# Handing out the sort's pieces beside the mean layer by their duration instead of by their number

## What is computed

```python
def _L0_gnn_ref(feature, src, dst, W):
    msgs = feature[src]
    summed = jax.ops.segment_sum(msgs, dst, num_segments=N_NODES)
    deg = jax.ops.segment_sum(jnp.ones_like(dst, dtype=feature.dtype), dst, num_segments=N_NODES)
    agg = summed / jnp.maximum(deg, 1.0)[:, None]
    return jax.nn.relu(agg @ W.T) + feature
...
def _L1_gnn_ref(x, edge_index, ...):
    nodes = jnp.concatenate([src, dst]); nbr = jnp.concatenate([dst, src])
    order = jnp.lexsort((nbr, nodes))
    nbrs = nbr[order].reshape(N, deg)
    h = _layer(h, nbrs, ...)          # uses w = _evolution_row(deg, tr, ti)
```

## Time and profile before

| | |
|---|---|
| median of 3 runs | 10004.24 us (9991.14 to 10006.8) |
| profiled execution, first to last instruction (its span) | 9988.2 us |
| profiled execution's own time | not listed apart from the span; the span lies 16.0 us under the median and within the spread of the runs but for 2.9 us |
| busy share of the span | PE 78%, DVE 80%, ACT 60%, POOL 70% |
| first gather of the mean issued | 366.7 us |
| last gather of the mean issued | 2516.4 us |

### The profile page before, as it was taken

The page is one execution under the profiler, slowest core; times in us unless marked ns, Lnnn a source line. Parts: engine busy times, 40 slices in busy tenths (PEclk is TensorE's granted clock), DMA queues, the critical chain, the costliest instruction groups (busy, mean ns, idle before and its releaser), DMA issues.

```text
span 9988.2 us, 178573 instructions
## 1 busy us (share of the span) xinstructions
PE 7824.2 (78%) x39865; PEld 6121.3 (61%) x39865; DVE 7971.0 (80%) x24833; ACT 5963.0 (60%) x18344; POOL 6961.9 (70%) x7476
## 2 busy tenths in 40 slices
PE   4444555555799999898889989888888888848887
PEld 4333444444477777777677777666666666636665
DVE  7787556555878887999967768788888888899999
ACT  6777777777877774111100006688888888846665
POOL 0466777777078887777678877566666666649995
PEclk6555555555899999999999999855565565557876
DMA  2222222222588888887766662322222222210000
GB/s 52 54 48 48 53 53 53 53 53 53 189 253 239 243 238 267 287 289 280 247 250 224 224 214 61 81 49 49 49 50 49 49 50 49 50 28 1 1 1 27
DMA packets 530133, 1151.52 MB, mean 115 GB/s; under 512 B 147134, under 2 KB 398210, under 8 KB 508750
## 3 DMA queue, kind: packets, MB, share of 16 engines
q0 software_dynamic: 241872, 477.23, 19.9%
q10 hardware_dynamic: 22752, 517.02, 13.2%
q1 hardware_dynamic: 264478, 145.85, 5.5%
HBM read 886.72 MB, written 259.31 MB: 115 GB/s over the span
## 4 chain that ended last, share of the span: by engine, by line
DVE 24%; POOL 23%; PE 22%; issue 14%; ACT 11%; DVEq 3%; DMA 2%; SPq 1%; ACTq 0%; POOLq 0%
POOL onehot L2185 9%; PE bank L1413 7%; POOL step_data L1743 7%; POOL step_data L1449 4%; PE bank_tile L2042 3%; POOL gather_ring L1449 3%; ACT onehot L1028 2%; DVE keys L1099 2%; DVE keys L1108 2%; ACT onehot L1026 2%; PE bank L1039 2%; DVE keys L1471 2%; DVE arena L1072 2%; PE bank_tile L2052 2%; DVE keys L2022 2%
## 5 line engine op out<-in xcount | busy, mean ns | idle before, releaser
L1014 POOL DMA_INDIRECT gather_ring<-mean_rows,step_data x1660 | 1596.1, 961 | 784.3 <-PE bank L1039 288.2
L1039 PE MATMUL bank<-gather_ring,onehot 128*128 128x130 f32 x3320 | 1042.1, 460 | 1053.0 <-DVE arena L1072 724.8
L1413 PE MATMUL bank<-arena 128*128 128x384 bf16 x8526 | 1628.5, 330 | 30.4 <-DMA arena<-split_out 26.9
L1413 PE MATMUL bank<-arena,keys 128*128 128x384 bf16 x8526 | 1623.5, 330 | 11.8 <-DMA arena<-split_im 11.8
L1039 PEld LDWEIGHTS bank<-gather_ring,onehot 128*128 128x128 f32 x3320 | 805.8, 306 | 1279.1 <-issue 851.6
L1413 PEld LDWEIGHTS bank<-arena 128*128 128x128 bf16 x8526 | 1178.9, 139 | 289.8 <-issue 47.5
L1413 PEld LDWEIGHTS bank<-arena,keys 128*128 128x128 bf16 x8526 | 1177.4, 138 | 270.5 <-issue 24.7
L1743 POOL DMA_INDIRECT step_data<-next_rows,window_idx x896 | 1045.9, 1167 | 351.1 <-issue 263.9
L1449 POOL DMA_INDIRECT step_data<-hidden,window_idx x888 | 1060.9, 1195 | 293.9 <-issue 265.9
L1966 POOL DMA_INDIRECT gather_ring<-attention_rows,step_data x834 | 786.8, 943 | 435.5 <-PE bank_tile L2042 228.6
L1966 POOL DMA_INDIRECT keys<-attention_rows,step_data x826 | 779.3, 943 | 388.0 <-PE bank_tile L2042 227.1
(11 more groups left out here) (350 smaller groups left out, 20302.8 us busy)
## 6 DMA issues: line engine op xcount, KB each, us to landing
keys<-count_rows ACTq DMA_DIRECT2D x50, 3136.0 KB
arena<-count_rows ACTq DMA_DIRECT2D x50, 3136.0 KB
count_rows<-arena ACTq DMA_DIRECT2D x26, 3136.0 KB
count_rows<-keys ACTq DMA_DIRECT2D x26, 3136.0 KB
gather_ring<-mean_rows,step_data POOLq DMA_INDIRECT x1660, 2.5
step_data<-next_rows,window_idx POOLq DMA_INDIRECT x896
step_data<-hidden,window_idx POOLq DMA_INDIRECT x888
gather_ring<-attention_rows,step_data POOLq DMA_INDIRECT x834
```

The costliest lines, as they stand in the source:

```text
L1014: e.indirect_dma_start(ring_at(rings.slot(name, i), SUM_COLS, SUMS - 1), None, rows, bass.IndirectOffsetOnAxis(src_idx[:, i:i + 1], 0), bo ...
L1039: e.matmul(pass_bank[i % N_SUM_BANKS][:, 0:SUMS], onehot[:, i % STEP_SLOTS, :], ring_at(rings.slot(name, i), SUM_COLS, SUMS), start=True, ...
L1413: m = e.matmul(pass_bank[n % 2][:, 0:SPLIT_COLS], counts[t % 2][:, :, h], split[:, h, :], start=(h == 0), stop=(h == NODE_TILES - 1))
```

## The change

A list of costs, one for each side piece, takes the place of their number: 66 for a stage and for the masking piece, 15 for an evolution piece, 8 for a turn (and for the 16 last pieces), 24 for a rescale; the sum is 14,116. weave_timed puts in the next piece as soon as the cost handed out so far is behind the share of places that have passed.

```diff
+STAGE_COST, SHORT_COST, TURN_COST, RESCALE_COST = 66, 15, 8, 24
...
+def weave_timed(main, side, main_total, costs):
+
+    total, spent, at = sum(costs), 0, 0
+    for done, _ in enumerate(main, 1):
+        while at < len(costs) and spent * main_total < done * total:
+            next(side)
+            spent, at = spent + costs[at], at + 1
+    for _ in side:
+        pass
...
-SORT_STAGES = len(SORT) + 1 + DEG // 4 + GROUPS // 4
+EVO_STAGES = 10
+SIDE_COSTS = [SHORT_COST] * EVO_STAGES + [
+    {"stage": STAGE_COST, "turn": TURN_COST, "rescale": RESCALE_COST}[row[0]] for row in SORT] + [
+    STAGE_COST] + [TURN_COST] * (DEG // 4 + GROUPS // 4)
...
-        weave(sum_vector(e, "mean", 0, regs), itertools.chain(evo_vector(e), sort_vector(e)), STEPS, EVO_STAGES + SORT_STAGES)
+        weave_timed(sum_vector(e, "mean", 0, regs), itertools.chain(evo_vector(e), sort_vector(e)), STEPS, SIDE_COSTS)
...
-        weave(sum_tensor(e, "mean", 0), itertools.chain(range(EVO_STAGES), sort_tensor(e)), STEPS, EVO_STAGES + SORT_STAGES)
+        weave_timed(sum_tensor(e, "mean", 0), itertools.chain(range(EVO_STAGES), sort_tensor(e)), STEPS, SIDE_COSTS)
...
-        weave(sum_scalar(e, 0), itertools.chain(evo_scalar(e), sort_scalar(e)), STEPS, EVO_STAGES + SORT_STAGES)
+        weave_timed(sum_scalar(e, 0), itertools.chain(evo_scalar(e), sort_scalar(e)), STEPS, SIDE_COSTS)
```

More of the change, by code:

```diff
@@ L880, in prep_scalar_program @@
         some_of(counting, HIST_GROUPS + 1)
-    EVO_STAGES = 10
     def evo_vector(e):
```

## The result

| | before | after |
|---|---|---|
| median of the runs | 10000.3 us (9991.14 to 10006.8, 4 runs) | **9957.81 us** (9954.06 to 9961.2, 4 runs) |
| profiled span | 9988.2 us | 9952.3 us |
| gathers, first to last start | 366.7 to 2516.4: 2149.7 us | 371.4 to 2479.8: **2108.5 us** |
| over POOL's own pace (2071.3 us) | 78.4 us | 37.2 us |

Ratio **0.9958, interval 0.9944 to 0.9972**: faster by 42.5 us by the medians, 45 were forecast (9959 us, from a kernel before at 10004.2). The start of the first gather moves between 366 and 372 us, and what follows the last gather between 7467 and 7484 us, from one profile to another with nothing changed there. So each kernel is judged by the span of its gathers, which neither touches: it fell by 41.2 us.

A forecast was written before the change was run, and what follows sets the result against it. The mean was taken as bound by DVE in its dense stretch, then by POOL's gathers at 1.2485 us. Gain 49.3 - 3.6 - 0.5 = 45 us, 10004.2 to 9959 us; own range 9949 to 9972, 8 in 10 within 9946 to 9984.

The forecast's parts named there:

- the 52.5 us over it: Gathers from 494.2 to 983.7 us: excess over POOL's pace, forecast to go except 3.2 us, gain 49.3 us.
- The two rescales of the dense stretch: Two rescales hidden in POOL's wait come out of cover, 2 x 1.59 = 3.2 us.
- The bursts: Turns in bursts of eight, one a step: the ring of 14 slots covers their lag, 0 us lost.
- gather 29: Start, evolution in 16 places then a stage: this gather waits for step 15's product, 3.6 us lost (0 to 8).
- Stages 7.76 places apart ... ACT needs 7.6.: Stage cycles: DVE needs 8.25 us, ACT 7.6, POOL offers 9.69, so POOL's pace ends last in all 190.
- stage cycles don't fit: Rival at the ACT copy, DVE stage, adds, PE cycle: slower from 10.04 us a cycle, 10025 us; chance 0.04.
- the tight cycle of 6.69 us: Stage cycle before the change, 641.33 to 648.02 us, said to contain every hand-over; 2.9 further steps give 8.3 us.
- After it each cycle wins 1.4 us of lag back: Stage cycles after the stall at the start: lag drains by 1.4 us in each.
- peak under 9: PE's lag in the tightest pair of bursts stays under 9 us; the ring covers 17.5 us.
- the spare 8 us: Spare ring at the bursts, the argument against the rival that bursts empty the ring (28 us lost; bursts' chance 0.12).
- DVE works 4.5: Stage behind a burst: DVE works 4.5 us after ACT's copies, 8.9 us with hand-overs, 3.9 lost.
- The end.: End of the mean: entries' store issued about 1.4 us after the last gather, 0.5 us lost (0 to 4).

The follow-up runs named there:

- the run that opened the circle as well: Changed kernel with rescales on ScalarE at cost 36, SHORT_COST 41 (evolution spread) and HOT_LEAD 2: 9929.12 us, ratio 0.9931 to the kernel before.

## Why the prediction was right, and where its working was not

**Right.** POOL's pace is what the dense stretch now goes by; the 52.5 us over it are gone but for 1.5. The two rescales of the dense stretch were paid as forecast (14 stretched gathers are over the pace now). The bursts cost nothing. One stall lies at gather 29, 4.9 us by 3.6 forecast. Nothing follows the last add but what followed before.

**The sum.** 37.2 us are left over the pace, where 32.7 followed from the forecast (78.4 less 45.7). Term by term it is 37.6 by 32.2: 3.1 more for the rescales (1.81 us each, I took the 1.59 of one row; the twelve of before average 1.64), 1.3 at gather 29, 2.2 in small stalls, 1.0 less at the first gathers and 0.2 less at the masking. So the gathers' span shrank by 41.2, not 45.7. The last of them is at 2479.8 rather than the 2471 forecast: 4.5 us are this difference, and the first began 4.7 us later in this profile. That start, and 0.7 us after the last gather, is why the profiled span fell by only 35.9 us while the medians differ by 42.5.

**"Stages 7.76 places apart ... ACT needs 7.6."** The step that failed. It added up ACT's busy time and took each engine for itself. The circle costs 9.68 us, 2.1 of it ACT's wait for PE, and just fits into the 9.69 that POOL offers. The 1.4 us a cycle that I counted as spare were not there, so that the gain came in full at this place is luck. My rival "stage cycles don't fit", at 0.04, was much nearer than its chance said: one place less between stages brought the kernel back to 0.9996. Its argument against, that the tight cycle of 6.69 us contains every hand-over, was wrong. In that cycle of before the copy for the next stage was this:

```profile
645.97 1.88 ACT L1175 ACTIVATE bank_tile<-keys 128x2048 f32<-128x2048 f32 x1 [1.15 <-DVE keys L1108]
```

It began 0.11 us behind the stage's end (645.86). With under five places from stage to stage no one-hot that waits for a product stood ahead of it, so the cycle didn't contain the walk by add, product and one-hot at all.

**"After it each cycle wins 1.4 us of lag back", "peak under 9".** Neither holds. The lag stayed near 18.5 us for 450 steps and reached 20.7 at the first pair of bursts (steps 630 to 657), where the ring begins to run dry: the spare 8 us weren't there. From step 900 on it peaked at 13.2, once the turns had let it drain. The bursts were harmless for another reason than the one given. They cost PE less than I took (1.28 us a step, then 0.66), and a burst holds no stage.

**"DVE works 4.5" in the first stage and behind a burst.** Two stages of the 190 hold DVE for 7.5 to 7.6 us, with four operations of 2.0 in place of 1.22: the first, and the one between the bursts of the tightest pair. L1107 in the trace of before has such operations (its longest is 2030 ns); I read the median. At the start it hardly showed, because the evolution ended 5.0 us before gather 29 was due, where my walk had 2.4. The two errors nearly cancel, so 4.9 us for 3.6 is partly luck.

**The end.** The store was issued before the last gather and not after, for 0 us in place of 0.5.

The granted clock of 500 to 950 us is 0.55 where I expected 0.50, with PE busier (197 us for 184). It is no single place: in slices of 50 us it is 0.51 to 0.57, where before has 0.50 in every slice.

## What to carry to other kernels

Where engines run in a fixed order and hand slots round in a circle, add up the circle (who must finish before whom, with every hand-over), not only each engine's busy time; here it was 4.02 us + 0.73 a place, 9.7 us in all, where DVE's own work came to 8.3 and ACT's to 7.6. How far ahead a small producer runs is part of that circle: running five ahead in a ring of eight put its work behind the very product that a long operation held up, two ahead freed it. And before moving work to a less busy engine, see what is queued behind it there: the rescales gained 25 us and lost more on ACT, and the gain showed only in the run that opened the circle as well.

## What was not expected of the hardware

- Minimum and maximum of 128x1024 float32 take 1.93 to 2.04 us in the two stages in which the elements of the keys lie 16 bytes apart (distance 1 in runs of 2). They take 1.22 us in the other stages of the same form, in which at least two neighbours among the elements lie 4 or 8 bytes apart. The Trainium skill (SBUF — State Buffer, the note on cachelines under "Door 1: The DMA port swizzle") says that SBUF has 16-byte lines and each access that crosses to a new one pays. These durations agree.
- A gather issued beside a rescale on DVE lengthens by 1.67 to 2.08 us, beside the same rescale on ACT by nothing. The two gathers that began before DVE's rescale ended 0.12 us behind it, the twelve that began during it 0.81 us behind it. So what a rescale costs depends on where it falls between two gathers. The Trainium skill (SBUF — State Buffer, "SBUF: two separate sides") has the port pair that DVE and GpSimd share taken for a whole instruction by a DVE operation in a 2-port mode, and ACT never waiting for anyone. The ends of the gathers agree with the first, the run with the rescales on ACT with the second; no row names the mode of DVE's rescale.
- PE's granted clock rises within a burst of turns, while no pause lies between its instructions: it is 0.50 (1.2 GHz) from 1170 to 1173 us and 1.00 (2.4 GHz) from 1174 to 1176, and four transposes take 1.06 us at 1171.31 and 0.60 us at 1174.58.
